# Attention and int8 layer on one core: one transfer for both max rows, merged rounding passes, and loads moved between ScalarE's and SyncE's queues

## What is computed

```python
Q, K, V = (proj(Wq), proj(Wk), proj(Wv))          # einsum('oc,bct->bto') split in heads
att = einsum('bhqd,bhkd->bhqk', Q, K) / sqrt(32) + b[0]
m = mask[:, None, None, :]
att = softmax(att * m + (1.0 - m) * -1e30, axis=-1)
y = einsum('bhqk,bhkd->bhqd', att, V)             # back to (B, C, T)
scale = max(absmax(y over T), 1e-7) / 127         # one per row
q = clip(round(y / scale), -128, 127)
out = x + float16((q @ weight.T) * scale * w_scale + bias)
```

## Time and profile before

| | before |
|---|---|
| runs, us | 2412.73, 2415.08, 2416.57 (median 2415.08) |
| profiled execution, us | 2414.74 (its span 2412.8; 1.94 lie outside it) |
| granted TensorE clock | 0.995 |
| busy, share of span | TensorE 97%, GpSimd 71%, VectorE 65%, ScalarE 56% |
| first unit of `attend` to the end | about 1,850 of the 2,412.8 us |
| DMA engines busy from 600 to 2340 us | 0.88 of the time |

### The profile page before, as it was taken

How to read it: one execution, slowest core, us unless ns; L and a number is a source line. 1 busy time by engine, 2 the same in 40 slices (tenths; PEclk the granted TensorE clock), 3 DMA queues, 4 the chain that set the end, 5 groups by cost and what they waited for, 6 DMA issues and landing times.

```text
span 2412.8 us, 36511 instructions
## 1 busy us (share of the span) xinstructions
PE 2342.3 (97%) x11840; PEld 1320.4 (55%) x11872; DVE 1561.4 (65%) x1683; ACT 1343.3 (56%) x2536; POOL 1725.1 (71%) x740
## 2 busy tenths in 40 slices
PE   8999999999999999999999999999999999999996
PEld 7888888885444444444444444444444444444442
DVE  3311111147787777777787877777778777787771
ACT  3322222215666666666666666666666666666664
POOL 3322233324888888888888888888888888888887
PEclk9999999999999999999999999999999999999998
DMA  6645554467888888898988998888988888989971
GB/s 244 255 187 216 200 200 184 175 213 165 194 185 194 193 191 199 195 195 196 203 194 191 195 194 193 190 188 191 196 195 184 197 190 195 201 193 194 204 151 47
DMA packets 152569, 462.60 MB, mean 192 GB/s; under 512 B 15592, under 2 KB 51432, under 8 KB 128304
## 3 DMA queue, kind: packets, MB, share of 16 engines
q0 software_dynamic: 27216, 198.19, 42.9%
q10 hardware_dynamic: 48864, 129.19, 20.5%
q1 hardware_dynamic: 76416, 134.34, 15.5%
HBM read 161.51 MB, written 100.93 MB: 109 GB/s over the span
## 4 chain that ended last, share of the span: by engine, by line
PE 77%; DMA 10%; POOL 5%; issue 3%; ACT 2%; ACTq 1%; SPq 1%; DVE 1%; POOLq 0%; DVEq 0%
PE score L725 18%; PE pv L754 16%; PE ring L131 15%; PE ring L324 11%; PE score L324 9%; DMA q_stack<-max_lo 8%; PE ring L788 4%; POOL acc L1026 4%; PE pv L324 3%; PE ring L769 1%; ACT probs L836 1%; DMA k_stack<-bias_part 1%; ACTq L119 1%; DMA probs<-probs 1%; PE ring L779 1%
## 5 line engine op out<-in xcount | busy, mean ns | idle before, releaser
L836 ACT ACTIVATE probs<-score 128x512 f32<-128x512 f32 x2048 | 1076.8, 604 | 590.6 <-PE score L725 539.8
L140 DVE TENSOR_REDUCE neg_max<-ring 128x1 f32<-128x1024 f32 x1024 | 1210.8, 1220 | 260.3 <-PE ring L131 251.8
L725 PE MATMUL score<-q_stack,k_stack 100*128 100x512 f32 x2048 | 878.1, 430 | 36.4 <-DMA q_stack<-max_lo 21.1
L1026 POOL TENSOR_TENSOR acc<-acc,probs 128x2048 f32<-128x2048 f32 x189 | 876.8, 4639 | 21.5 <-DMA probs<-probs 12.9
L131 PE MATMUL ring<-k_stack,q_stack 98*128 98x512 f32 x2048 | 811.4, 396 | 2.8 <-DMA k_stack<-bias_part 1.8
L725 PEld LDWEIGHTS score<-q_stack,k_stack 100*128 100x128 f32 x2048 | 386.1, 189 | 530.1 <-ACT probs L836 370.9
L754 PE MATMUL pv<-probs,v_in 128*32 128x512 f32 x4096 | 546.3, 605 | 0.0
L131 PEld LDWEIGHTS ring<-k_stack,q_stack 98*128 98x128 f32 x2048 | 389.3, 190 | 73.4 <-DVE neg_max L140 6.8
L1026 POOL TENSOR_TENSOR acc<-probs 128x2048 f32<-128x2048 f32 x63 | 288.7, 4582 | 191.5 <-DMA probs<-probs 121.9
L526 POOL TENSOR_TENSOR q_stack<-x_raw,k_stack 128x1024 fp32r<-128x1024 f32 x28 | 67.7, 2455 | 292.2 <-ACT k_stack L402 292.2
L1010 POOL DMA_DIRECT2D probs<-probs x189 | 172.8, 914 | 52.2 <-PE pv L754 48.8
(11 more groups left out here) (101 smaller groups left out, 1950.0 us busy)
## 6 DMA issues: line engine op xcount, KB each, us to landing
probs<-probs POOLq DMA_DIRECT2D x189, 1024.0 KB, 9.1
q_stack<-qk_part ACTq DMA_DIRECT2D x183, 256.0 KB, 7.9
k_stack<-qk_part ACTq DMA_DIRECT2D x90, 512.0 KB
qk_part<-part_hi SPq DMA_DIRECT2D x64, 512.0 KB, 2.6
qk_part<-part_lo SPq DMA_DIRECT2D x64, 512.0 KB, 3.5
v_steps<-v_out SPq DMA_DIRECT2D x64, 256.0 KB, 2.2
v_out<-x ACTq DMA_DIRECT2D x32, 512.0 KB, 5.6
out<-v_out SPq DMA_DIRECT2D x64, 256.0 KB, 2.0
```

Source lines behind the costliest of these rows:

```text
L140: nc.vector.tensor_reduce(neg_max[:, pair // CHUNK, pair % CHUNK:pair % CHUNK + 1], ring[:, :], AX_X, ALU.max, negate=True).then_inc(neg_m ...
L725: pe.matmul(score[score_bank(t)][:, :], k_stack[par][0:ROWS, h, kt * P:(kt + 1) * P], q_stack[par][0:ROWS, half, h, :], start=True, stop=T ...
L836: nc.scalar.activation(probs[:, kt, h, :], score[score_bank(t)][:, :], ACT.Exp).then_inc(exp_done, 1)
L1026: nc.gpsimd.tensor_tensor(acc[:, half, :, :], first, probs[:, tile, :, :], ALU.add).then_inc(acc_done, 1)
```

## The change

- **Max rows.** ScalarE doubles the 16 maxima to 32 columns (`double_max`, behind units 21 and 53), the turned tile has 32 rows, and two constant columns (`marks`) let one pass of each engine leave the high parts in rows 0 to 15 and the low parts in rows 16 to 31. One transfer then fills both rows of the stack.
- **Rounding.** One pass of 1024 columns at unit 39 in place of two of 512, and one at unit 43 for the integers.
- **ScalarE's loads.** Keys at units 0, 3 and 7; queries at 33, 36, 40, 42, 45 and 48.
- **SyncE's queue.** It now issues the bias rows at the start of a step, and behind unit 31 the values of the next step and then the residual rows. The second half of the output rows moves to the next step.

```diff
+LOAD_K, LOAD_Q1, LOAD_Q0 = (0, 3, 7), (33, 36, 40), (42, 45, 48)
-MAX_ROWS = 16 * 2
+MAX_ROWS = 16
...
+def double_max(nc, act, neg_max, s, chunk, neg_max_done, doubled):
+
+    act.wait_ge(neg_max_done, PAIRS * s + CHUNK * (chunk + 1))
+    nc.scalar.activation(neg_max[:, chunk, CHUNK:2 * CHUNK], neg_max[:, chunk, 0:CHUNK], ACT.Copy).then_inc(doubled, 1)
+
...
+    pe.wait_ge(doubled, 2 * s + chunk + 1)
+    pe.transpose(buf[0:2 * CHUNK, 0:P], neg_max[:, chunk, :], ident[:, :]).then_inc(maxT_done, 1)
...
-    nc.scalar.activation(max_hi[:, chunk, :], buf[0:CHUNK, 0:P], ACT.Copy).then_inc(max_hi_done, 1)
+    nc.scalar.activation(max_parts[:, chunk, :], buf[0:2 * CHUNK, 0:P], ACT.Identity, scale=marks[:, 1:2]).then_inc(max_hi_done, 1)
...
+    nc.vector.scalar_tensor_tensor(max_parts[:, chunk, :], buf[0:2 * CHUNK, 0:P], marks[:, 0:1],
+                                   max_parts[:, chunk, :].bitcast(F32), ALU.mult, ALU.subtract).then_inc(max_lo_done, 1)
...
-    for part, rows in ((0, max_hi), (1, max_lo)):
-        dst = q_stack[par][ROW_MAX + part:ROW_MAX + part + 1, chunk, :, :]
-        sp.dma_start(dst.bitcast(F32), rows[:, chunk, :].bitcast(F32)).then_inc(max_rows[chunk], 16)
+    dst = q_stack[par][ROW_MAX:ROW_MAX + 2, chunk, :, :]
+    sp.dma_start(dst.bitcast(F32), max_parts[:, chunk, :].bitcast(F32)).then_inc(max_rows[chunk], 16)
...
+                if ahead and not first:
+                    sp.wait_ge(score_done, UNITS * s)
+                    for part in range(2):
+                        load_bias(sp, bias_d, k_stack, s + 1, 1 - par, part, k_loaded)
+                if not isinstance(s, int) or s >= 2:
+                    store_out(s - 2, 1)
                 if main:
-                    sp.wait_ge(max_hi_done, 2 * s + 2)
                     sp.wait_ge(max_lo_done, 2 * s + 2)
-                    store_max(sp, q_stack, max_hi, max_lo, par, 1, max_rows)
+                    store_max(sp, q_stack, max_parts, par, 1, max_rows)
+                    sp.wait_ge(score_done, UNITS * s + UNITS // 2)
...
+                    sp.dma_start(v_in[:, 1 - par, :, :], v_d[bass.ds(s + 1, 1)].rearrange("o p a c -> (o p) a c")).then_inc(v_loaded[1 - par], 16)
+                if prev:
+                    wait(sp, out_stored, 32 * (s - 1))
+                    sp.dma_start(res[:, :], x[bass.ds((s - 1) * P, P), :]).then_inc(res_loaded, 16)
...
+                if s > 0 and ahead and t in LOAD_K:
+                    if t == LOAD_K[0]:
+                        act.wait_ge(score_done, UNITS * s)
+                    load_k(act, qk_d, k_stack, s + 1, 1 - par, LOAD_K.index(t), k_loaded)
+                if ahead and t in LOAD_Q1:
+                    load_q(act, qk_d, q_stack, s + 1, 1 - par, 1, LOAD_Q1.index(t), q2_loaded)
+                if t in LOAD_Q0 and s + 2 < STEPS:
                     act.wait_ge(score_done, UNITS * s + UNITS // 2)
-                    load_q(act, qk_d, q_stack, s + 2, par, 0, t - 38, q1_loaded)
+                    load_q(act, qk_d, q_stack, s + 2, par, 0, LOAD_Q0.index(t), q1_loaded)
```

More of the change, by code:

```diff
@@ L490, in _ @@
             batch(0, 0)
+            dve.wait_ge(ident_set, 1)
+            nc.vector.tensor_reduce(marks[:, 0:1], ident[0:2 * CHUNK, 0:CHUNK], AX_X, ALU.max).then_inc(marks_set, 1)
+            dve.wait_ge(marks_set, 1)
+            nc.vector.tensor_scalar(marks[:, 1:2], marks[:, 0:1], -2.0, 1.0, ALU.mult, ALU.add).then_inc(marks_set, 1)
+            dve.wait_ge(marks_set, 2)
+            nc.vector.tensor_scalar(marks[:, 0:1], marks[:, 0:1], -1.0, 1.0, ALU.mult, ALU.add).then_inc(marks_set, 1)
             dve.wait_ge(small_loaded, 32)
@@ L666, in _ @@
                 load_bias(sp, bias_d, k_stack, 1, 1, part, k_loaded)
-            step(0, 0, prev=False)
-            step(1, 1)
-            step(2, 0)
-            with sp.Fori(1, STEPS // 2 - 1) as pair:
-                step(2 * pair + 1, 1)
-                step(2 * pair + 2, 0)
-            step(STEPS - 1, 1, ahead=False)
-            step(STEPS, 0, main=False, ahead=False)
+            all_steps(sp, step)
+            store_out(STEPS - 1, 1)
             sp.wait_ge(out_stored, 32 * STEPS)
@@ L775, in turn_q @@
                     pe.wait_ge(fw_done, 1)
[L776 removed]
+                pe.wait_ge(q_done, s + 1)
                 buf16 = buf[:, :].bitcast(BF16)
@@ L841, in take_y, with round_rows @@
                 nc.scalar.activation(y_raw[:, half, :], pv[:, :], ACT.Copy).then_inc(y_raw_done, 1)
[L843 to L845 removed]
+            def round_rows(s):
+                if s == 0:
                     act.wait_ge(const_set, 3)
[L847 removed]
                 act.wait_ge(inv_done, s + 1)
[L849 removed]
@@ L851, in make_ints @@
-            def make_ints(s, half):
-                cols = slice(half * N, (half + 1) * N)
-                act.wait_ge(rounded, 2 * s + half + 1)
+                nc.scalar.activation(y[:, :], y[:, :], ACT.Identity, bias=magic[:, 0:1], scale=inv_scale[:, 0:1]).then_inc(rounded, 1)
+            def make_ints(s):
+                act.wait_ge(rounded, s + 1)
                 wait(act, qT_done, s)
-                nc.scalar.activation(q_int[:, cols], y[:, cols], ACT.Identity, bias=magic[:, 1:2]).then_inc(q_done, 1)
@@ L857, in loads @@
-            def loads(s, par, t, prev, ahead):
-                if s > 0 and ahead and t < 3:
-                    if t == 0:
-                        wait(act, score_done, UNITS * s)
-                    load_k(act, qk_d, k_stack, s + 1, 1 - par, t, k_loaded)
-                if s > 0 and ahead and t in (4, 5):
-                    load_bias(act, bias_d, k_stack, s + 1, 1 - par, t - 4, k_loaded)
-                if ahead and t == 16:
-                    if s == 0:
-                        for i in range(2):
-                            act.wait_ge(v_stored[i], 16 * B * TT // 2)
-                    wait(act, pv_done, QH * TT * s)
-                    act.dma_start(v_in[:, 1 - par, :, :], v_d[bass.ds(s + 1, 1)].rearrange("o p a c -> (o p) a c")).then_inc(v_loaded[1 - par], 16)
-                if prev and t == 22:
-                    load_res(s - 1)
-                if ahead and t in (33, 34, 36):
-                    load_q(act, qk_d, q_stack, s + 1, 1 - par, 1, (33, 34, 36).index(t), q2_loaded)
-                if ahead and t in (38, 39, 40) and not (isinstance(s, int) and s + 2 >= STEPS):
+                nc.scalar.activation(q_int[:, :], y[:, :], ACT.Identity, bias=magic[:, 1:2]).then_inc(q_done, 1)
```

103 lines of the change are left out of this document (51 added, 52 removed).

## The result

| | before | after |
|---|---|---|
| median, us | 2415.36 (4 runs) | 2472.26 (4 runs) |
| lowest to highest, us | 2412.73 to 2416.57 | 2470.86 to 2484.28 |
| profiled execution's span, us | 2412.8 | 2471.6 |
| granted TensorE clock | 0.995 | 0.976 |

The changed kernel takes 1.0248 times as long as the kernel before, 95% interval 1.0215 to 1.0281. The prediction was 2402.3 us in a range from 2383 to 2420: wrong in its sign, 70 us above the forecast and 52 us above the range.

What follows compares the result with a forecast made beforehand. GpSimd's ring of its own work and pair transfers was taken as the bound: -0.55 + 0 + 0.1 + 0.1 = -0.35 us a step, x 30 = -10.5, with -2.3 in the tail, from 2415.08 to 2402.3 us, range 2383 to 2420.

Steps and rivals of the forecast that it cites:

- (c): Values and residual issued behind unit 31, close to transfer 0.2: +0.1 us a step, bounds 0 and +0.6.
- (b): First link, transfer 0.0 to the first add: no sooner landing, 0; at most -0.5 us a step.
- The ring: GpSimd's own work and the transfers it issues set each step, mean 57.27 us; stalls on TensorE or ScalarE count nothing.
- (a): Values and residual leave the stretch between transfers 0.0 and 0.1: second link -0.55 us a step, bounds 0 and -0.9.
- (d): Query loads at units 42, 45 and 48, ahead of transfer 1.0: +0.1 us a step, bounds 0 and +1.4.
- Max rows: One joint transfer saves at most TensorE's wait of 0.63 us a step, which lies outside the ring: 0.
- More waits of unit 20 than 17: Unit 20's exponential should wait for GpSimd in more steps than 17, longer in total.
- Tail: After the last step: GpSimd's pass about 2.0 us earlier and rounding 0.3, together -2.3 us.
- The slower rival: Query loads queue behind held-up 0.2 and make transfer 1.0 late: +0.95 us a step, 2441 us; chance 0.12.
- The rival of TensorE as the bound: TensorE sets the time, so its stalls count: 27 us and the tail, 2386 us; chance 0.07.

Runs made afterwards that it cites:

- e6: Kernel before with only two numbers changed: ScalarE issues the values at unit 57 instead of 16 and the residual at 38 instead of 22; 2407.72 us.
- e8: Changed kernel with values and residual still behind unit 31, but issued by ScalarE in place of SyncE; 2459.96 us.
- e9: Changed kernel with the values back on ScalarE at unit 16 and the residual alone behind unit 31, also on ScalarE; 2404.75 us.
- e10: Changed kernel with the residual back on ScalarE at unit 22 and the values alone behind unit 31, also on ScalarE; 2393.16 us.
- e16: Kernel before with one number changed: ScalarE issues the values at unit 31 in place of 16; 2408.06 us.
- e1: Kernel before with only the values' and residual's loads moved, issued by SyncE behind unit 31; 2474.25 us.
- e3: Changed kernel with the query loads back at units 33, 34, 36, 38, 39 and 40; 2460.55 us.
- e2: Changed kernel with values and residual back on ScalarE's queue at units 16 and 22; 2421.77 us.
- e11: Changed kernel with GpSimd's order altered: pair transfer 0.2 and the second add stand ahead of the second half's normalisation; 2411.09 us.
- e12: The GpSimd order of e11 applied to the kernel of e4; 2416.57 us.
- e13: The GpSimd order of e11, with values and residual both issued by ScalarE at unit 27, where it issues transfer 0.2; 2419.66 us.
- e4: Changed kernel with the residual at unit 38 and the values at unit 57, both issued by ScalarE; 2399.24 us.

## Why the prediction was wrong

**The failing step is (c).** It gave the values and the residual behind unit 31 +0.1 us a step, at most +0.6. The link takes +2.07 us (11.44 against 9.37), 62 us over 30 turns; against the 9.64 of a link without this wait it is +1.80, or 54. Two things in it were off. The price: 1.9 us for the two loads was read from 0.1 behind 0.0, as a difference to a span that ran from a bias row's landing to an add, which isn't the time of a pair transfer. e6, which moves these two loads alone, has the price there: 0.1 lands 10.0 us after its issue in the kernel before and 7.4 without them, so they cost 2.7. Beside 0.2 they cost 3.4 (11.9 against 8.5), in e8 2.7. And I gave half of that by a guess at how much would stand in front, though unit 31 and the issue of 0.2 fall together; the loads start 0.4 us before it and 0.3 behind it. The form of the step was right: the price counts from where the third later add wants the transfer, 10.2 us after the issue (the prediction had 9.9), and with one load (e9, e10) it is 0, as (c) had it.

**(b), no gain at the first link, and its limit of 9.1 us.** Both wrong. The link fell to 7.22. The first add waits for a sum of two halves back, not for the one behind unit 23, so nothing there held it; and the values did hold 0.0 up: e16, which moves them alone in the kernel before, has 8.94 for 9.58, and with both loads moved (e6) it is 8.83. The rest of the fall, to 7.2 to 7.9, is seen only where 0.2 is late (after, e1, e3, e8): GpSimd then reaches 0.0 later in the stream of units, with more of the key loads over. That reason is argued, not tried. The sum behind unit 23 is waited for one instruction later, by the normalisation through its factor. More than the whole of the 2.36 gained went there, +3.03. In the earlier trace rows that wait had no bracket, and I read this as "no gap that another engine decides", so the sum had no term for it; it had 0.64 us of room (factor 8.27, normalisation begun 8.91 after the last add, from the kernel before's timelines).

**The second loop has two speeds**, which I had not seen. At full clock the factor comes 8.1 us after the last add. When unit 20 has waited long and TensorE been idle behind it, the clock is at times halved and it takes 9.2 to 11.1. Two neighbouring steps of e1 and one with the lower level throughout, the clock third from the end:

```profile
1383.60:1388.60 5.00, 4.37 (x25) 1.95 (x26) 2.94 (x6) 3.20 (x7) 5.00 (x3) 1.00 0.68 139
1442.20:1447.20 5.00, 4.28 (x19) 0.75 (x19) 1.50 (x2) 2.33 (x5) 5.00 (x3) 0.69 0.64 131
1502.30:1507.30 5.00, 4.63 (x19) 1.00 (x19) 1.50 (x2) 2.06 (x5) 4.71 (x3) 0.50 0.69 141
```

The normalisation of the first half, which begins as the last add ends, and the factor's pass, in the first two:

```profile
1383.19 1.53 POOL L1040 TENSOR_TENSOR y<-y_raw,factor 128x512 f32<-128x512 f32 x1
1390.61 0.70 DVE L925 STREAM_TRANSPOSE factor<-recips 128x512 f32<-128x512 f32 x1
...
1441.85 1.55 POOL L1040 TENSOR_TENSOR y<-y_raw,factor 128x512 f32<-128x512 f32 x1
1450.83 0.70 DVE L925 STREAM_TRANSPOSE factor<-recips 128x512 f32<-128x512 f32 x1
```

7.4 us at 2.4 GHz throughout, 9.0 with the clock at 0.69. The length of unit 20's wait alone doesn't decide it: in the changed kernel the clock stayed at 1.00 behind one of 3.98 us and had a mean of 0.66 behind one of 3.09. Over 28 steps of e1, 18 at full clock have the factor after 8.06 us (7.84 to 8.40) and 10 at a lower one after 9.80 (9.22 to 10.85). In the changed kernel, with 20 such steps of 28, the mean is 9.57, 1.5 us a turn above 8.1. The four runs of e1 fall in nearly the same order: 2459.2 us at a mean clock of 0.987, 2468.1 at 0.984, 2480.4 and 2483.8 at 0.978 and 0.979. That the clock makes the delay is read from such pairs; no run took the clock away.

**Point by point, the rest.** The ring as such: right, and the turns carry the loss. (a): right in sign and too large. The link fell by 0.62 for the 0.55 forecast, but 0.27 of it comes back in the next (9.64 for 9.37), which leaves 0.35; the three adds of the earlier trace rows that showed no wait also took 14.29 us against 13.90 in the earlier trace rows. (d): +0.05 in the changed kernel, within its bounds, but +0.6 in e2, so its +0.1 was small for the kernel that I had in mind. Max rows: right, 18.8 to 0.3 us and worth nothing by itself. More waits of unit 20 than 17: right, 31. Tail: -1.8 for -2.3. The residual's wait is gone and the normalisation waits for the factor, as said, but counted from the last step's transfer 0.0 it begins 1.1 us earlier, not 2.0:

```profile
2451.57 1.26 POOL L1055 TENSOR_TENSOR y<-y_raw,factor 128x512 f32<-128x512 f32 x1 [1.16 <-DVE factor L940]
```

The slower rival had the two loads hold up 0.2, but let only 1.0 pay for it, at 7.0 us in the changed kernel no later than before. The rival of TensorE as the bound has at most this truth, that GpSimd waits for the sum through the factor: 16.6 us in e10, against 0.5 before.

**Open**: how the loss of e8 over e10 (2.3 us a turn) divides between the late 0.2 (+1.25) and the late factor (+2.33, less what 0.0 gives, -1.10), since each kernel had both or neither.

## What to carry over

Price a load by what it meets at the moment of its issue, and compare the landing with the work that covers it: up to the cover it costs nothing, beyond it everything, so two loads can cost 60 us where each alone costs none. An instruction without a bracket is not one without a limit: before counting a gain in a ring, look up for every instruction in it how long ago its other inputs came, since the gain ends there. When a view says who ended a wait, set the start beside the landings before believing it: here 70 us of waits for transfers stood under two other engines' names. When GpSimd's order is free, put the instruction that needs another engine's answer behind one that doesn't.

## What the hardware showed

- A pair transfer of 1 MB with accumulation took 6.9 us in its quick places (1.0 in the kernel before, 0.0 in the changed one); transfer 0.2 took 8.3 to 8.5 with the query loads alone issued behind it, 9.2 and 9.6 with one load of 512 KB issued within about 1 us of it, 10.2 with 768 KB and 11.2 to 12.0 with 1 MB.
- TensorE's granted clock was 0.50, that is 1.2 GHz, over 5 us in a step where ScalarE had waited 3.87 us for the last add; it was also 1.00 behind waits of up to 3.60 us in the same run, and of up to 3.98 us in the changed kernel.
- Transfer 1.0 landed after 8.4 us on average in the turns of e11, e12 and e13 in which one query load of 256 KB was issued about 0.4 us behind it, and after 7.3 us in e4, where the last one came 0.6 to 1 us ahead.
